# Six score tiles moved from the second softmax to the projections, in a fused attention and feed-forward kernel

## What is computed

```python
qk = einsum('bhqd,bhkd->bhqk', Q, K)                 # Q from layernorm(x), K and V from ctx
probs = softmax(qk / sqrt(dk))                       # the FIRST softmax: only its statistics are used
feats = [mean(scores), mean(max(scores)), mean(var(probs))]        # one triple for each head
t = exp(clip(mlp(feats)))                            # a small MLP with two gelus
attn = softmax(qk / (2 * t))                         # the SECOND softmax
x = x + tanh(g_xattn) * (attn @ V @ Wo.T + bo)
x = x + tanh(g_ffn) * bitlinear(gelu(bitlinear(layernorm(x), w1)), w2)
```

## Time and profile before

| | |
|---|---|
| time, median of 3 runs (lowest, highest) | 1405.53 us (1403.91, 1407.44) |
| time of the profiled execution | 1404.38 us |
| its span in the profile | 1402.2 us |
| PE busy | 1209.3 us, 86% |
| DVE busy | 1107.2 us, 79% |
| ACT busy | 921.9 us, 66% |
| POOL busy | 422.6 us, 30% |
| mean granted TensorE clock | 0.939 |

### The profile page before, as it was taken

How to read it: one execution, slowest core, us unless ns; L and a number is a source line. 1 busy time by engine, 2 the same in 40 slices (tenths; PEclk the granted TensorE clock), 3 DMA queues, 4 the chain that set the end, 5 groups by cost and what they waited for, 6 DMA issues and landing times.

```text
span 1402.2 us, 23484 instructions
## 1 busy us (share of the span) xinstructions
PE 1209.3 (86%) x6684; PEld 443.9 (32%) x6684; DVE 1107.2 (79%) x2054; ACT 921.9 (66%) x1527; POOL 422.6 (30%) x399
## 2 busy tenths in 40 slices
PE   5635769999999899999999899998999899869958
PEld 2201311344224432344224431344224431233224
DVE  7297869887898869887898869887898879983246
ACT  5553769664985669664985669664985679645713
POOL 4289374510253114510253114510353101100210
PEclk9857879999999999999999999999999999889979
DMA  8710231102112221102112221102112210001000
GB/s 296 217 60 8 54 83 52 28 20 69 54 47 46 47 78 47 29 18 69 54 46 46 47 78 46 39 17 68 46 47 45 47 61 1 1 1 61 1 0 30
DMA packets 35475, 73.73 MB, mean 53 GB/s; under 512 B 7952, under 2 KB 7952, under 8 KB 34832
## 3 DMA queue, kind: packets, MB, share of 16 engines
q1 hardware_dynamic: 35344, 72.13, 17.9%
HBM read 38.39 MB, written 8.39 MB: 33 GB/s over the span
## 4 chain that ended last, share of the span: by engine, by line
PE 52%; DVE 26%; ACT 9%; issue 9%; POOL 1%; SPq 1%; DMA 1%; DVEq 1%; ACTq 0%; POOLq 0%
PE b_ps L1251 11%; DVE stat L920 7%; DVE nmax L915 5%; PE o_ps L1449 5%; PE o_ps L1251 5%; ACT region L750 5%; PE z_ps L1251 4%; PE o_ps L1291 4%; PE b_ps L1278 4%; PE a_ps L1272 4%; ACT etile L733 3%; PE b_ps L1428 2%; PE z_ps L1449 2%; PE b_ps L1439 2%; PE z_ps L1302 2%
## 5 line engine op out<-in xcount | busy, mean ns | idle before, releaser
L733 ACT ACTIVATE etile<-a_ps,nmax 128x512 f32<-128x512 f32 x512 | 369.6, 733 | 143.1 <-DVE nmax L915 143.0
L915 DVE TENSOR_REDUCE nmax<-a_ps 128x1 f32<-128x512 f32 x512 | 346.3, 678 | 59.6 <-PE a_ps L1272 55.8
L750 ACT ACTIVATE region<-b_ps,inv2t 128x512 f32<-128x512 f32 x512 | 353.3, 758 | 57.8 <-PE b_ps L1278 29.0
L920 DVE BATCH_NORM_STATS2 stat<-etile 128x6 f32<-128x512 f32 x512 | 348.2, 682 | 6.8 <-ACT etile L733 6.8
L1272 PE MATMUL a_ps<-kst,qst 96*128 96x512 f16 x512 | 204.3, 403 | 61.4 <-ACT etile L733 46.5
L1278 PE MATMUL b_ps<-qst,kst 97*128 97x512 f16 x512 | 196.0, 393 | 23.6 <-ACT region L750 16.5
L1291 PE MATMUL o_ps<-region,vbuf 128*32 128x512 f32 x1024 | 140.2, 620 | 8.2 <-ACT region L750 6.3
L1278 PEld LDWEIGHTS b_ps<-qst,kst 97*128 97x128 f16 x512 | 49.3, 97 | 302.2 <-ACT region L750 279.9
L1302 PE MATMUL z_ps<-region,ones 128*32 128x512 f32 x1024 | 137.1, 608 | 8.4 <-DVE region L939 8.4
L653 POOL TENSOR_TENSOR region<-region 128x512 f16<-128x512 f32 x64 | 76.6, 1197 | 219.3 <-ACT region L783 219.1
L609 POOL TENSOR_TENSOR region<-region 128x512 f32<-128x512 f32 x32 | 40.9, 1277 | 312.8 <-DVE region L946 312.8
(11 more groups left out here) (278 smaller groups left out, 1961.4 us busy)
## 6 DMA issues: line engine op xcount, KB each, us to landing
kst<-region SPq DMA_DIRECT2D x96, 128.0 KB, 2.3
qst<-region SPq DMA_DIRECT2D x96, 128.0 KB, 2.3
xres<-in_x_dram SPq DMA_DIRECT2D x8, 1024.0 KB, 6.5
out_dram<-xres SPq DMA_DIRECT2D x32, 256.0 KB, 2.1
cin<-in_ctxT_dram SPq DMA_DIRECT2D x30, 256.0 KB, 2.7
cin<-in_x_dram SPq DMA_DIRECT2D x28, 256.0 KB, 2.7
kst<-in_f1T_dram SPq DMA_DIRECT2D x2, 1024.0 KB, 12.7
qst<-in_f2T_dram SPq DMA_DIRECT2D x2, 1024.0 KB, 10.7
```

Of the source, the lines that this page charges most:

```text
L733: nc.scalar.activation(etile[:, k % E_SLOTS, :], a_ps[k % A_BANKS][:, :], ACT.Exp, bias=nmax[:, slot_of(n), t:t + 1], scale=1.0).then_inc( ...
L750: nc.scalar.activation(probs[:, s % 2, g, :], b_ps[g % 2][:, :], ACT.Exp, scale=inv2t[:, slot:slot + 1]).then_inc(b_exp, 1)
L915: vec.tensor_reduce(nmax[:, slot_of(k // T), k % T:k % T + 1], a_ps[k % A_BANKS][:, :], AX.X, ALU.max, negate=True).then_inc(a_max, 1)
L920: vec.bn_stats(stat[:, slot_of(k // T) * T + k % T, :], etile[:, k % E_SLOTS, :]).then_inc(a_stat, 1)
```

## The change

`A_PLAN` is used by the turns 1 to 6. The other two plans, for turn 0 and turn 7, stay.

```diff
-A_PLAN = (40, (2, 2, 2, 2, 1, 1, 1, 1, 1, 1, 1, 1, 2, 2, 2, 2))
+A_PLAN = (34, (2, 2, 2, 2, 2, 2, 2, 1, 1, 2, 2, 2, 2, 2, 2, 2))
 A_PLAN_0 = (28, (3, 3, 3, 3, 0, 0, 0, 0, 3, 3, 3, 3, 3, 3, 3, 3))
```

## The result

The changed kernel takes 1413.03 us, median of 6 runs (1410.44 to 1417.92); the kernel before took 1406.26 us in the 6 runs shown beside it. The medians lie 6.8 us apart. The ratio, which compares runs made beside each other and so is not exactly the quotient of the medians, is 1.0055, 95% interval 1.0038 to 1.0072: the change makes the kernel slower, by half a per cent. The forecast was 1414 us from 1405.53.

The account below looks back on a forecast made before the run. ACT paces the sets, with PE and DVE near their limit; PE bounds the K, W and Q points. Per turn -3.8 + 3.7 + 1.5 = +1.4 us, six turns +8.4: 1414 us from 1405.53, range 1404 to 1421.

Parts of the forecast that it names:

- Sets, 3.8 us saved a turn: Sets part: two-tile sets take 3.51 us instead of 3.76, PE setting the pace; 3.8 us saved a turn, ends 2.4 and 4.5.
- The chain behind set 8: After set 8: DVE's fixed row of work up to PE's denominators product stays 5.73 us; the sets around it lose 0.5.
- W, 0.65: W points: three more PE matmuls add 0.65 us a turn; DVE has slack and the last residual moves by 0.67.
- V, together with W 3.7: W0 to Q0: six matmuls, 1.3 us, plus a PE stall growing from 0.86 to about 3.3 us; adds 3.7 a turn.
- The clock, 1.5: Q points: a half-clock stretch of 3.4 us behind the new PE gap costs 1.5 us a turn, upper end 2.6.
- The premise: Feed-forward part: PE idles about 3 us and the granted clock is then 0.50 for 3.40 us, in all six turns.
- The rule of the Trainium skill: A kernel keeps the high clock if idle gaps stay below a length longer than this one; then -0.1 us a turn.
- Sum, +1.4 a turn, +8.4: Each turn: -3.8 in the sets, +3.7 from W0 to Q0, +1.5 for the clock; +8.4 us over six turns.
- No fall of the clock: Gap in front of Q0 costs no clock: -0.1 us a turn, 1402 to 1408 us, centre 1405; chance 0.22.
- The stall that does not grow: V points: V2's first maximum is ready in time and ACT copies on time; 2.5 us a turn gained, 1390.5 us; chance 0.05.
- The sets that save less: Sets: ACT and DVE keep the pace, saving 2.4 instead of 3.8; 1422 us; chance 0.15 with late DVE at W.
- a DVE late at the W points: W3: slack only 0.1 to 0.2 us, lateness passes to Q0; 0.5 us gives 1417; chance 0.15 with smaller sets saving.

Follow-up runs that it names:

- copy_first: Changed kernel, with ACT copying each V product before the exponentials of its point in turns 1 to 6: 1403.50 us, 0.9981 of the kernel before.
- quant_late: Changed kernel, with DVE quantising the residual behind both tiles of V2 instead of ahead of them: 1416.47 us, 1.0079 of the kernel before.
- v_only: Kernel before, with only the three tiles at V1, V2 and V3 moved, 37 staying in the sets: 1421.93 us, ratio 1.0113.
- plan_v0: Changed kernel's 34 set tiles, but V1 to V3 have one tile each, W3 and V0 two, Q1 three: 1394.82 us, 0.9921 of the kernel before.
- pe_filled: Changed kernel plus fourteen unused constant matmuls on PE between last V product and wait for copies, turns 1 to 6: 1404.65 us, 0.9986 of kernel before.

## Why the prediction was right, point by point

- **Sets, 3.8 us saved a turn.** 4.1 in the mean (66.00 to 61.87). The pace was taken rightly: values products follow each other by 3.51 us (522.43, 525.93, 529.44 in turn 3). The chain behind set 8 stayed at 5.73 us (545.18 to 550.91), as assumed; the wait at its end was put at 1.7 and is 1.55; that for the last values product stayed, 0.83. What the forecast did not have is the clock inside the sets part. It is below 1.00 in the opening of four turns of the kernel before (65.87 to 66.86 us, where the other two take 65.16 and 65.36) and of two turns of the changed one (62.18 and 62.91, where the other four take 61.33 to 61.75). Between the turns at the full clock the saving is 3.7 us; the other 0.4 are fewer low stretches, which nothing in the forecast foresaw.
- **W, 0.65.** 0.67, and DVE did keep up: the last residual starts 0.20 us behind the first transpose of x, as before (598.75 and 598.95; now 601.16 and 601.36).
- **V, together with W 3.7.** 0.67 + 3.10 = 3.8. The gap was put at 3.3 and is 3.18. The chain was read as it runs: second tile of V1, quantising, V2's maximum, exponential, copy. V2's first maximum was put 1.87 us later than before, and is 1.85 later, counted from the first W product (586.87 to 610.91 before, 588.61 to 614.50 now). copy_first shortens the gap by changing the order on ACT alone, and quant_late moves the long wait to V3's tile together with the quantising; v_only shows the gap with V's tiles alone; plan_v0 takes it away.
- **The clock, 1.5.** 1.63 in the mean of Q (15.46 - 13.83), in five turns of six, and 0.4 more in the rest. pe_filled shows the cause. The mechanism is right; that the size fits so well is in part luck. It was one stretch of 3.4 us behind each gap; in fact two turns had twice that, three had one, and one had none, and in four of the five it began while PE still stood in the gap. Gaps of the same length cost the Q points 0.9 us in the mean in v_only (three turns of six) and 1.2 in quant_late (four of six). The premise, that the gap in the feed-forward part is followed by a low clock in six turns of six, holds in three of the ten kernels, the one before among them; over all ten it is 48 turns of 60. The rule of the Trainium skill that was set against it, in "TensorE: Matmul & The Clock Gate", section "HAM oscillation — how this bites in real kernels", would have kept the high clock; the trace does not agree, with gaps of 3.18 us.
- **Sum, +1.4 a turn, +8.4.** +1.66 in the profiled pair, +6.8 us in the medians, which is 1.1 a turn. The size was a bit high; the runs differ among themselves by 4.0 us before and 7.5 after, and how many stretches at half clock an execution gets is likely part of that: the two slowest runs of the changed kernel, 1417.92 and 1414.52 us, have the lowest mean clocks, 0.929 and 0.931, and the fastest, 1410.44, the highest, 0.941.
- **Rivals.** No fall of the clock gives pe_filled's 1404.65; it was put at 1405. The stall that does not grow did not come: V2's first maximum starts 1.85 us later, as said, and from L982 on (605.43) DVE runs without a gap up to it, as the prediction argued. The sets that save less did not come either (61.87 us), nor a DVE late at the W points.

Not settled: why the clock falls behind a gap in one turn and not in the next. The same gap of 3.2 us is followed by none (turn 3), one or two low stretches. All six turns issue the same instructions, so it hangs on something that differs between them and that no run here fixed. Nor was it looked into why the shift ahead of turn 1 differs from kernel to kernel.

## What to carry to other kernels

A plan that balances busy time between stages can lose by order alone: before moving a tile, list on each in-order engine what stands behind it, and ask whether another engine waits for that. Six tiles cost 6.8 us at one set of points and saved 11.8 at another. A longer PE gap can cost more than itself: here 2.3 us of stall came with 1.6 of lower clock (0.9 and 1.2 in two other kernels with such a gap), so a stall of 3 us is to be priced with a stretch at half clock behind it in most turns (12 of 18 here), and one of 2 us in some (5 of 18); filler matmuls in the gap gave 9.7 us back, though taking the gap away is better, 18 us in plan_v0.

## What the runs showed of the hardware that I had not expected

How often a PE gap was followed by a stretch at half clock, counted over the turns 1 to 6 of all ten kernels (a stretch counts when it begins in the gap or at most 1.4 us behind it):

| gap | where | low stretch behind it |
|---|---|---|
| 0.85 to 1.07 us | in front of Q0 | 0 of 30 |
| 1.40 to 1.56 | behind set 8 | 0 of 54 |
| 1.75 to 1.79 | behind set 8 | 6 of 6 |
| 2.00 | inside the Q points | 3 of 12 |
| 2.19 to 2.20 | in front of Q0 | 2 of 6 |
| 3.18 to 3.33 | in front of Q0 | 12 of 18 |
| 2.98 to 3.16 | feed-forward part | 48 of 60 |

So a gap of under 2 us in the middle of a busy stretch can already be followed by a stretch at half clock, and one of over 3 us need not be: the length of the gap alone does not decide it. And 14 matmuls, 3.19 us long, in the place of a gap of 3.18 us were enough to keep 1.00 at the Q points in all six turns.
